# Expert layers: zeroing moved behind the norm, the chosen rows by two 16-bit products, and ACT and DVE in turn for the copies

## The reference

```python
grouped = x.reshape(B, g, t, d)                     # groups of t = 32 tokens
logits = einsum('bgtd,des->bgtes', grouped, controller) + tie
perm = (logits == max(logits over t))               # each of 128 expert sets takes one token of a group
dispatched = einsum('bgtd,bgtes->bgesd', grouped, perm)
inner = relu(einsum('bgesd,desf->bgesf', dispatched, f1) + bias)
intermediate = einsum('bgesf,esfd->bgesd', inner, f2)   # the second layer adds a bias b2 here
out = einsum('bgesd,bgtes->bgtd', intermediate, perm)
```

## Time and profile before

| | us |
|---|---|
| median of 3 runs | 2502.02 |
| lowest and highest run | 2498.89, 2502.21 |
| profiled execution, its own time | 2494.57 |
| its span in the trace | 2492.8 |
| granted PE clock, mean over the span | 0.979 |

### The profile page before, as it was taken

One profiled execution on the slowest core, in us unless ns is written; L12 is line 12 of the kernel. 1 busy time (PEld: TensorE's weight loads), 2 busy tenths in 40 slices (PEclk: granted clock), 3 DMA queues, 4 the chain that ended last, 5 costly groups with the idle time before them and its releaser, 6 DMA issues. The chain is left out here.

```text
span 2492.8 us, 68127 instructions
## 1 busy us (share of the span) xinstructions
PE 2303.6 (92%) x27961; PEld 1491.0 (60%) x27961; DVE 1864.0 (75%) x2822; ACT 1673.9 (67%) x3037; POOL 1846.9 (74%) x1105
## 2 busy tenths in 40 slices
PE   2999999999999999999999999999999998689987
PEld 1365665566566655665666556655666556558875
DVE  8877777887787878877877787878777761467754
ACT  4677777777677777776777677767777776246642
POOL 1798888989888988898889888888889998120000
PEclk9899999999999999999999999999999999889988
DMA  2612223132413141414131413141313000600000
GB/s 87 164 40 57 72 79 99 49 83 67 111 38 96 56 122 36 97 56 122 36 93 60 118 40 94 61 117 40 93 61 88 2 2 10 186 10 2 2 4 9
DMA packets 107639, 165.57 MB, mean 66 GB/s; under 512 B 23544, under 2 KB 97216, under 8 KB 102208
## 3 DMA queue, kind: packets, MB, share of 16 engines
q1 hardware_dynamic: 104032, 157.12, 23.0%
q10 hardware_dynamic: 3296, 4.10, 0.5%
HBM read 99.22 MB, written 61.97 MB: 65 GB/s over the span
## 5 line engine op out<-in xcount | busy, mean ns | idle before, releaser
L608 POOL TENSOR_TENSOR att_prob_low<-att_prob 128x1024 f16<-128x1024 f32 x960 | 1765.5, 1865 | 230.0 <-PE all_banks L728 126.4
L885 ACT ACTIVATE att_prob<-all_banks 128x512 f32<-128x512 f32 x1888 | 1070.7, 591 | 366.3 <-PE all_banks L693 247.7
L979 DVE TENSOR_REDUCE att_part<-all_banks 128x2 f32<-128x1024 f32 x800 | 946.5, 1218 | 197.9 <-PE all_banks L653 197.9
L714 PE MATMUL all_banks<-att_v,att_prob 128*128 128x129 f16 x5664 | 584.1, 221 | 2.8 <-DVE shared_att L1003 0.6
L714 PEld LDWEIGHTS all_banks<-att_v,att_prob 128*128 128x128 bf16 x5664 | 414.6, 98 | 238.0 <-issue 10.8
L728 PEld LDWEIGHTS all_banks<-att_v,att_prob_low 128*128 128x128 f16 x7552 | 328.8, 98 | 138.4 <-POOL att_prob_low L608 18.7
L674 PE MATMUL all_banks<-att_qc,att_kc 128*128 128x512 f16 x1056 | 401.3, 380 | 0.0
L675 PE MATMUL all_banks<-att_qd,att_kd 128*128 128x512 f16 x1056 | 401.0, 380 | 0.0
L728 PE MATMUL all_banks<-att_v,att_prob_low 128*128 128x65 f16 x7552 | 386.0, 194 | 13.4 <-POOL att_prob_low L608 13.4
L718 PE MATMUL all_banks<-att_v,att_prob 128*128 128x64 f16 x1888 | 371.2, 197 | 0.0
L716 PE MATMUL all_banks<-att_v,att_prob 128*128 128x65 f16 x1888 | 365.9, 194 | 0.0
(11 more groups left out here) (304 smaller groups left out, 3074.8 us busy)
## 6 DMA issues: line engine op xcount, KB each, us to landing
att_kc<-k_high SPq DMA_DIRECT2D x30, 928.5 KB, 10.8
att_v<-v_all SPq DMA_DIRECT2D x14, 1870.5 KB
v_all<-att_stage_v SPq DMA_DIRECT2D x98, 258.0 KB, 2.4
att_kd<-k_low SPq DMA_DIRECT2D x16, 928.5 KB, 15.0
k_high<-att_stage_h SPq DMA_DIRECT2D x98, 128.0 KB, 1.7
k_low<-att_stage_l SPq DMA_DIRECT2D x98, 128.0 KB, 1.9
att_kd<-k_low SPq DMA_DIRECT2D x16, 208.0 KB, 15.7
prep_ctx<-in_ctx SPq DMA_DIRECT2D x5, 640.0 KB, 9.1
```

What stands on the lines that cost most here:

```text
L608: pool.tensor_tensor(prob_low[g % NL][:, 0:w], p[:, 0:w], p.bitcast(BF16)[:, 1:2 * w:2], op=ALU.subtract).then_inc(low_split, 1)
L714: pe.matmul(O[:, q, :], w, v[:, e, t, :], start=first, stop=False, skip_group_check=True)
L885: act.activation(prob[g % NP][:, i * BANK:(i + 1) * BANK], S[n % 3], ACT.Exp, scale=SCALE)\
L979: dve.tensor_reduce(parts[:, n:n + 2], pers.banks[:, 4 + 2 * pair:6 + 2 * pair, :], axis=AX.X, op=ALU.max)\
```

## The change

In both expert layers:

- POOL waits for the transposes of the normalized tiles before it zeroes `pick`. `pick` is now F16 and is zeroed through a F32 view of the same bytes, 2048 elements for each partition. After it POOL writes `n_l`, then zeroes `hidden`.
- `n` is split in two F16 parts: `n_h`, a copy on ACT, and `n_l = n - n_h`, a subtraction on POOL. PE makes each row product of two 16-bit products into the same bank in place of one float product.
- ACT copies the front half of the picks and DVE the back half; ACT copies the row products of tiles 0 to 3 and DVE those of 4 to 7.
- In the result loop ACT copies the even pieces and DVE the odd ones.

In the second layer alone: the down bias is no longer added in the result loop. PE transposes it with `up_bias`, ACT copies it to `down_bias_t`, and DVE adds it while it copies the down products to `result_t`, which ACT copied before.

```diff
-        pick = sc.sb("pick", [P, TOKEN_TILES, W, ES])
+        pick = sc.sb("pick", [P, TOKEN_TILES, W, ES], F16)
+        n_h = sc.sb("n_h", [P, TOKEN_TILES, D], F16)
+        n_l = sc.sb("n_l", [P, TOKEN_TILES, D], F16)
...
-            pool.memset(pick[:, :, :, :], 0.0).then_inc(s["pick_zeroed"], 1)
+            pool.wait_ge(s["transposed"], 2)
+            pool.memset(pick[:, :, :, :].rearrange("p t w c -> p (t w c)").bitcast(F32), 0.0).then_inc(s["pick_zeroed"], 1)
+            pool.wait_ge(s["n_high"], 1)
+            pool.tensor_tensor(n_l[:, :, :], n[:, :, :], n_h[:, :, :], op=ALU.subtract).then_inc(s["n_low"], 1)
...
+            act.activation(n_h[:, :, :], n[:, :, :], ACT.Copy).then_inc(s["n_high"], 1)
             act.wait_ge(s["bias_transposed"], 1)
+            if second:
+                act.activation(down_bias_t[:, :], B[6][:, EXPERTS:EXPERTS + ES], ACT.Copy).then_inc(s["bias_copied"], 1)
             act.activation(up_bias_t[:, :], B[6][:, 0:EXPERTS], ACT.Copy).then_inc(s["bias_copied"], 1)
...
-            for i in range(2):
-                act.wait_ge(s["pick_transposed"], i + 1)
-                for g in range(W):
-                    r = slice(g * GROUP, (g + 1) * GROUP)
-                    last = act.activation(pick[r, 4 * i:4 * i + 4, g, :],
-                                          B[i][r, :].rearrange("p (t c) -> p t c", c=ES), ACT.Copy)
-                last.then_inc(s["pick_copied"], 1)
+            act.wait_ge(s["pick_transposed"], 1)
+            for g in range(W):
+                r = slice(g * GROUP, (g + 1) * GROUP)
+                last = act.activation(pick[r, 0:4, g, :], B[0][r, :].rearrange("p (t c) -> p t c", c=ES), ACT.Copy)
+            last.then_inc(s["pick_front"], 1)
+            for t in range(4):
+                act.wait_ge(s["took"], t + 1)
+                act.activation(taken_t[:, W * t:W * (t + 1), :], B[2 + t][:, :].rearrange("p (g c) -> p g c", c=ES),
+                               ACT.Copy).then_inc(s["took_front"], 1)
...
-            for k in range(EXPERTS // W):
-                act.wait_ge(s["down_done"], k + 1)
-                act.activation(result_t[:, k * 4 * SETS:(k + 1) * 4 * SETS, :],
-                               B[k % 4][:, :].rearrange("p (c g) -> p c g", g=GROUPS), ACT.Copy)\
-                   .then_inc(s["down_read"], 1)
+            if not second:
+                for k in range(EXPERTS // W):
+                    act.wait_ge(s["down_done"], k + 1)
+                    act.activation(result_t[:, k * 4 * SETS:(k + 1) * 4 * SETS, :],
+                                   B[k % 4][:, :].rearrange("p (c g) -> p c g", g=GROUPS), ACT.Copy)\
+                       .then_inc(s["down_read"], 1)
+            for k in range(0, GROUPS // 4, 2):
+                act.wait_ge(s["result_transposed"], k + 1)
+                act.activation(result[:, 4 * k:4 * k + 4, :], B[4][:, :].rearrange("p (g d) -> p g d", d=D), ACT.Copy)\
+                   .then_inc(s["result_even"], 1)
...
-            for t in range(TOKEN_TILES):
+            dve.wait_ge(s["pick_zeroed"], 1)
+            dve.wait_ge(s["pick_transposed"], 2)
+            for g in range(W):
+                r = slice(g * GROUP, (g + 1) * GROUP)
+                last = dve.tensor_copy(pick[r, 4:8, g, :], B[1][r, :].rearrange("p (t c) -> p t c", c=ES))
+            last.then_inc(s["pick_back"], 1)
+            for t in range(4, TOKEN_TILES):
                 dve.wait_ge(s["took"], t + 1)
                 dve.tensor_copy(taken_t[:, W * t:W * (t + 1), :], B[2 + t % 4][:, :].rearrange("p (g c) -> p g c", c=ES))\
-                   .then_inc(s["took_copied"], 1)
-            dve.wait_ge(s["bias_copied"], 1)
+                   .then_inc(s["took_back"], 1)
+            dve.wait_ge(s["bias_copied"], 2 if second else 1)
...
-            for k in range(GROUPS // 4):
+            if second:
+                for k in range(EXPERTS // W):
+                    c = slice(k * 4 * SETS, (k + 1) * 4 * SETS)
+                    dve.wait_ge(s["down_done"], k + 1)
+                    dve.tensor_tensor(result_t[:, c, :], B[k % 4][:, :].rearrange("p (c g) -> p c g", g=GROUPS),
+                                      spread_columns(down_bias_t[:, c], GROUPS), op=ALU.add).then_inc(s["down_read"], 1)
+            for k in range(1, GROUPS // 4, 2):
                 dve.wait_ge(s["result_transposed"], k + 1)
-                o = result[:, 4 * k:4 * k + 4, :]
-                i_ = B[4 + k % 2][:, :].rearrange("p (g d) -> p g d", d=D)
-                if second:
-                    if k == 0:
-                        dve.wait_ge(s["bias_in"], 32)
-                    b = down_bias[:, :].rearrange("p (one d) -> p one d", one=1).to_broadcast([P, 4, D])
-                    dve.tensor_tensor(o, i_, b, op=ALU.add).then_inc(s["result_copied"], 1)
-                else:
-                    dve.tensor_copy(o, i_).then_inc(s["result_copied"], 1)
+                dve.tensor_copy(result[:, 4 * k:4 * k + 4, :], B[5][:, :].rearrange("p (g d) -> p g d", d=D))\
+                   .then_inc(s["result_odd"], 1)
...
+            if second:
+                pe.transpose(B[6][:, EXPERTS:EXPERTS + ES], down_bias[:, :], ident[:, :])
             pe.transpose(B[6][:, 0:EXPERTS], up_bias[:, :], ident[0:EXPERTS, 0:EXPERTS]).then_inc(s["bias_transposed"], 1)
...
-                    pe.wait_ge(s["bias_copied"], 1)
+                    if k == 0:
+                        pe.wait_ge(s["bias_copied"], 2)
...
+            pe.wait_ge(s["n_low"], 1)
             for t in range(TOKEN_TILES):
-                if t % 4 == 0:
-                    pe.wait_ge(s["pick_copied"], t // 4 + 1)
+                if t == 0:
+                    pe.wait_ge(s["pick_front"], 1)
+                if t == 4:
+                    pe.wait_ge(s["pick_back"], 1)
                 if t >= 4:
-                    pe.wait_ge(s["took_copied"], t - 3)
-                pe.matmul(B[2 + t % 4][:, :], n[:, t, :], pick[:, t, :, :].rearrange("p g c -> p (g c)"),
-                          start=True, stop=True).then_inc(s["took"], 1)
+                    pe.wait_ge(s["took_front"], t - 3)
+                chosen = pick[:, t, :, :].rearrange("p g c -> p (g c)")
+                pe.matmul(B[2 + t % 4][:, :], n_h[:, t, :], chosen, start=True, stop=False)
+                pe.matmul(B[2 + t % 4][:, :], n_l[:, t, :], chosen, start=False, stop=True).then_inc(s["took"], 1)
...
-            pe.wait_ge(s["took_copied"], TOKEN_TILES)
+            pe.wait_ge(s["took_front"], 4)
+            pe.wait_ge(s["took_back"], TOKEN_TILES - 4)
...
-                        pe.wait_ge(s["result_copied"], k - 1)
+                        pe.wait_ge(s["result_odd" if k % 2 else "result_even"], k // 2)
...
-                    pe.wait_ge(s["result_copied"], k)
+                    pe.wait_ge(s["result_odd" if j % 2 else "result_even"], j // 2 + 1)
```

More of the change, by code:

```diff
@@ L1151, in stage_experts @@
         names = ("control_in up_in down_in bias_in tie_ready vec normalized transposed copied scored picked "
[L1152 removed]
+                 "pick_transposed pick_zeroed pick_front pick_back n_high n_low took took_front took_back up_done "
+                 "hidden_zeroed biased_ready "
                  "hidden_front hidden_back bias_transposed "
[L1154 removed]
+                 "bias_copied down_transposed down_copied down_done down_read result_transposed result_even result_odd "
                  "returned added stored").split()
```

3 lines of the change are left out of this document (1 added, 2 removed).

## The result

| | before, us | changed, us | ratio | 95% interval |
|---|---|---|---|---|
| first comparison, medians | 2500.45 | 2479.14 | 0.9920 | 0.9901 to 0.9938 |
| the same two again | 2495.56 | 2475.63 | 0.9917 | 0.9904 to 0.9931 |
| profiled execution, first comparison | 2494.57 | 2479.82 | | |

The ratios are estimated from all executions and not from the medians, so they are not exactly the quotients of the medians; one execution of `fill_down_before` (10931 us) was in the slow state and is left out of its ratio.

The account below looks back on a forecast made before the run. The prediction found no engine full and took the expert stages as a chain. Gains of 7.35 us in the first layer and 7.55 in the second, together 14.9, turned 2502.0 into 2487.1 us, range 2481 to 2494.

Parts of the forecast that it names:

- Norm: Start of both expert stages: DVE's L116 and L129 no longer wait out POOL's memsets, 8.7 us gained together.
- The hold of L1255: First layer's picks: POOL's subtraction holds this two-input DVE operation, 0.6 us lost; hidden in the second layer.
- Row products: Two 16-bit products replace each float product: 10.6 to 7.0 us in the first layer, 9.6 to 6.1 in the second.
- POOL's waits: POOL's later zeroing and making of `n_l`: ready at 2152.6, wanted by PE at 2155.9, so no cost.
- The turns of ACT and DVE: Copies shared by two engines: at half clock PE bounds the row products; result loop gains 0.1 us a layer.
- Together 0.4 us: Second layer, ahead of the `down` transposes: transposing `down_bias` and waiting for ACT's copy costs this, bounds 0.1 to 0.8.
- I leave the 4.2 us: PE's issue gap amid the first layer's up products, while bulk loads run: held unchanged, 2 us to each side.
- Either may come out either way: Down products, 7.41 us in the first layer and 10.35 in the second: held unchanged, 2.9 us each either way.
- the one thing that makes them longer: Down products, 7.41 against 10.35 us for the same 64 instructions: only a stretch at half clock lengthens them.
- Rival 2: Clock falls well: second layer's down products (2.9 us) and row products (1.2) at full clock; gain 19.0, 2483.0, chance 0.20.
- rival 1: First layer's down products begin at half clock (2.9 us), issue gap grows by 1; gain 11.0, 2491.0, chance 0.20.
- rivals 3, 4, 5 and 6: In order: `pick` zeroing slow (0.05); `hidden` zeroing holds DVE (0.05); norm's holds stay (0.04); PE's clock stays low, 2517.4 (0.03).

Follow-up runs that it names:

- fill_down_before: Kernel before plus 14 identity transposes on PE in its wait for `hidden` ahead of the down products of both layers: 2495.21 us, ratio 0.9990.
- fill_down: Changed kernel plus 14 identity transposes on PE in its wait for `hidden` ahead of both layers' down products: 2476.19 us, ratio 0.9920 to the kernel before.
- split_low: Changed kernel with POOL making `n_l` in two halves, each behind a half of DVE's `pick_t`: 2477.98 us, ratio 0.9925 to the kernel before.

## Why the prediction was wrong

The direction was right and the mechanism of most terms too; the size was not, and the range was too narrow. The steps that failed are three terms that the sum held still or had with the wrong sign: the issue gap, the down products' clock, and the second layer's way to its row products. Step by step, with the mean of the two profiles of each kernel:

- **Norm**: forecast 8.7, measured 4.3 + 4.5 = 8.7. Right, ACT's table load as the next in line included. With the memsets back it is held again.
- **The hold of L1255**: forecast 0.6, measured 0.85 and 0.45 on DVE and about 0.8 on the way to the first product. Right. The holds of 0.36 and 0.64 us in the second layer cost nothing, as said: PE is at the transposes of `down` there.
- **Row products**: forecast 3.6 and 3.5 less, measured 3.6 and 3.0. In the first layer the difference is right by luck: the forecast went from 10.6 to 7.0, the means from 9.86 to 6.26, and both ends were 0.7 us too high, since the stretch at half clock differs from profile to profile. In the second layer it was 3.4 us long, as forecast, but began 0.2 us behind the first product (2441.95 for 2441.74) and not a microsecond, so the fifth tile and the copies behind it came later: 6.65 us for 6.1. At full clock 5.19 and 4.98 were measured for the 4.9 forecast.
- **POOL's waits** and `n_low`: nothing, as forecast. The result loop: 0.1 a layer, as forecast. The turns of ACT and DVE: worth as little as forecast.
- **The second layer's way from transposes to row products**: forecast 0.4 us dearer, measured 0.6 cheaper. The wrong step is "Together 0.4 us": the bias did cost that (1.00 us from the first transpose of a bias to the first of `down`, 0.62 before), but I had not read that the diff takes seven waits off PE's way between the pieces (0.25 us, shown), and in both profiles the clock rose while the score products still ran (2.87 and 2.58 us for 3.49 and 3.51; seen, not tested).
- **"I leave the 4.2 us"**: the issue gap, the largest miss. It fell by 2.5 us in the up stage (13.8 to 11.3). I had bounded that with 2, and the argument (PE meets the loads 7 us earlier) held a gain and a loss for equal. That the loads make the gap is shown, and the trace shows what PE waits for, its instruction packet.
- **"Either may come out either way"**: the down stages. Mean 8.8 to 9.5 in the first layer, 11.05 to 9.0 in the second, 1.3 us less in sum. In the kernel before, the second layer's came out slow in all three profiles without fillers there (11.0, 11.1, 10.8). I took one profile's draw as a coin, where only repetition could have told. Why that layer's clock falls so regularly is open. And half clock is not "the one thing that makes them longer": in `fill_down` a gap of 1.48 us stood in them at full clock.

These three misses add 1.0, 2.5 and 1.3 us to 14.9, less 0.5 from the row products and 0.2 from the hold, and give 19.0; the stages of the profiles give 19.2 in the mean, the medians 20 to 21, and the rest is not assigned. **The range** failed for a reason of its own: its lower end of 2481 took 6 us off the forecast, while the text itself had up to 3.3 us in the row products, 2 in the gap and 2.9 in the down products, and nothing that kept them from coming together. Rival 2, whose gain of 19.0 is nearest to the result, is right in the number only: it wanted the second layer's down products at full clock, which came in one profile of two, and its row products too, which came in neither, and it had nothing for the gap. Of rival 1, one half came in one profile (the first layer's down products at half clock, 10.24 us) and the other not, since the gap shrank. The rivals 3, 4, 5 and 6 did not occur: `pick` took 1.80 us; nothing of DVE's was held by the zeroing of `hidden`, and in `split_low` DVE's copies out of PSUM lay beside it and took 2.79 us, as without it; the norm's holds went; and the clock came back.

## What to carry to other kernels

In a stage that is a chain, an engine's clock and its code loading are terms of the sum, not noise: list every wait in which PE stands, and ask of each edit whether it shortens that wait, before costing the instructions. Instructions that only fill time have to be loaded too, and can move such a wait to a dearer place. Keep long POOL memsets off any stretch where DVE has `tensor_scalar` operations in SBUF: the delay of one on eight elements was the rest of the memset, or of two. Two remedies that each measured 0 to 2 us were worth 10 together, so try them in pairs when one's cost is the other's cause.

## What the runs showed of the hardware

- A 128x8 `tensor_scalar` of DVE in SBUF was held to the end of a POOL memset: 0.80, 2.3, 2.5, and twice through two in a row, 5.97 and 6.04 us, where it takes 0.17. Beside the same memsets a 128x8 reciprocal took 0.20 us and a `tensor_reduce` of 512 columns 0.69, as elsewhere. A DVE operation with two SBUF inputs was not held by memsets (0.17) but by a POOL subtraction (1.54, 1.14 and 1.05 for 0.69). The Trainium skill (SBUF — State Buffer, Who interferes with whom) says that two SBUF inputs contend with a GpSimd instruction that reads SBUF and not with one that only writes, and that `tensor_scalar` can enter a two-port mode, in which whoever issues first has the shared ports for the whole instruction. These rows agree, but for the two long holds, in which DVE was not let in between the two memsets.
- PE stood 4.2 to 5.5 us in the middle of 256 small products with bulk loads under way (four profiles that came there late), 2.0 to 2.9 us in seven that came there earlier and 3.7 to 3.8 in three more, and 0 to 0.34 us without the loads. It went on 1.4 to 1.7 us after a 16 KB packet of an instruction queue had landed.
- A met wait instruction between PE's pieces cost about 0.07 us for two.
- With 14 or 22 transposes of 128 columns in PE's wait of 2.9 us, the granted clock of the 64 down products behind it was 1.00 in nine stages of ten and 0.96 in the tenth; without them it was 0.72 to 0.84 in 17 of 26. At 1.00 they take 7.4 us, at 0.72 10.4.
